# Keys and values of a fused decoder layer computed units ahead into a ring of six places

## The reference, cut to what matters

```
q, k, v = x @ Wq.T + bq, x @ Wk.T + bk, x @ Wv.T + bv         # 16 heads of 16
scores  = q k / 4, causal; only the 32 largest of a row are kept
x = layernorm(x + softmax(kept scores) v @ Wo.T + bo)
h = relu(x @ proj_in[e].T)            # 8 experts, 256 -> 512, every token
o = h @ proj_out[e].T                 # 512 -> 256
x = layernorm(x + sum_e gate[token, e] * o[e])   # gate from ctx_512 and itok
xq = 4-bit rounding of (x @ hadamard); wq = ternary weight
x = layernorm(x + xq @ wq.T)
```

## Time and profile before

| what | value |
|---|---|
| median of 3 runs | 617.47 us (616.04 to 617.79) |
| the profiled execution, its own time | 619.88 us |
| its span, first to last instruction | 618.1 us |
| TensorE (PE) busy | 551.0 us, 89% |
| VectorE (DVE) busy | 474.8 us, 77% |
| ScalarE (ACT) busy | 386.5 us, 63% |
| GpSimd (POOL) busy | 343.9 us, 56% |
| mean granted TensorE clock | 0.943 |
| mean DMA rate | 32 GB/s |

### The profile page before, as it was taken

One profiled execution on the slowest core, in us unless ns is written; L12 is line 12 of the kernel. 1 busy time (PEld: TensorE's weight loads), 2 busy tenths in 40 slices (PEclk: granted clock), 3 DMA queues, 4 the chain that ended last, 5 costly groups with the idle time before them and its releaser, 6 DMA issues. The chain is left out here.

```text
span 618.1 us, 20334 instructions
## 1 busy us (share of the span) xinstructions
PE 551.0 (89%) x7156; PEld 472.0 (76%) x7156; DVE 474.8 (77%) x2995; ACT 386.5 (63%) x909; POOL 343.9 (56%) x336
## 2 busy tenths in 40 slices
PE   5577658999899999999999999999999999989942
PEld 3455537888688888888888888888888888878831
DVE  1788988986888978798879887998799897543213
ACT  2677648676567566666767576766585767546520
POOL 2477555764447454754556455655554656656831
PEclk9967568999999999999999999999999999999985
DMA  8153330001000100002000100020001000000000
GB/s 243 37 181 116 108 103 2 3 2 53 3 2 3 46 26 3 3 3 70 3 1 21 53 3 2 3 71 1 3 3 54 3 3 1 20 1 2 19 0 17
DMA packets 20021, 19.88 MB, mean 32 GB/s; under 512 B 1744, under 2 KB 17872, under 8 KB 19920
## 3 DMA queue, kind: packets, MB, share of 16 engines
q1 hardware_dynamic: 19920, 18.59, 9.6%
HBM read 16.49 MB, written 2.10 MB: 30 GB/s over the span
## 5 line engine op out<-in xcount | busy, mean ns | idle before, releaser
L462 POOL TENSOR_TENSOR h_lo<-h_raw,h_hi 128x512 f16<-128x512 f32 x128 | 149.4, 1168 | 153.8 <-ACT h_raw L580 153.3
L769 PE MATMUL ps_o<-w_hi,h_lo 128*128 128x256 f16 x512 | 139.8, 273 | 5.2 <-POOL h_lo L462 3.6
L753 PE MATMUL ps_z<-x1t_hi,w_lo 128*128 128x256 f16 x512 | 140.4, 274 | 0.6 <-DVE x1t_lo L911 0.6
L753 PE MATMUL ps_z<-x1t_lo,w_hi 128*128 128x256 f16 x512 | 140.1, 274 | 0.0
L753 PE MATMUL ps_z<-x1t_hi,w_hi 128*128 128x256 f16 x512 | 140.0, 274 | 0.0
L769 PE MATMUL ps_o<-w_lo,h_hi 128*128 128x256 f16 x512 | 139.6, 273 | 0.0
L769 PE MATMUL ps_o<-w_hi,h_hi 128*128 128x256 f16 x512 | 139.6, 273 | 0.0
L855 DVE MATCH_REPLACE8 taken<-next,taken 128x48 f32<-128x48 f32 (+2 forms) x576 | 127.6, 233 | 0.2
L576 ACT ACTIVATE h_hi<-ps_z 128x512 f16<-128x512 f32 x128 | 75.9, 593 | 57.3 <-PE ps_z L753 56.4
L850 DVE MAX8 next<-taken 128x8 f32<-128x48 f32 (+2 forms) x576 | 95.9, 235 | 0.1
L483 POOL TENSOR_TENSOR acc<-go_sb,acc 128x512 f32<-128x512 f32 x56 | 71.1, 1270 | 35.9 <-ACT go_sb L590 35.7
(11 more groups left out here) (106 smaller groups left out, 993.5 us busy)
## 6 DMA issues: line engine op xcount, KB each, us to landing
w_raw<-in_w1t SPq DMA_DIRECT2D x8, 512.0 KB, 4.1
w_raw<-in_w2t SPq DMA_DIRECT2D x8, 512.0 KB, 5.2
xt_sb<-in_xt SPq DMA_DIRECT2D x8, 256.0 KB, 3.2
x_sb<-in_x SPq DMA_DIRECT2D x8, 256.0 KB, 3.2
out<-out_sb SPq DMA_DIRECT2D x8, 256.0 KB, 2.1
ctx_sb<-in_ctx_w SPq DMA_DIRECT2D x8, 128.0 KB, 2.4
itok_sb<-in_itok SPq DMA_DIRECT2D x8, 128.0 KB, 2.5
wq_sb<-in_wqt SPq DMA_DIRECT2D x1, 256.0 KB, 2.9
```

What stands on the lines that cost most here:

```text
L462: nc.gpsimd.tensor_tensor(h_lo[:, e % 2, 2 * z:2 * z + 2, :], h_raw[:, z, :, :], h_hi[:, e % 2, 2 * z:2 * z + 2, :], ALU.subtract)\
L753: last = pe.matmul(ps_z[z][:, d * UT:(d + 1) * UT], w[:, e, c, at:at + P], x[:, c, :], start=n == 0, stop=n == len(terms) - 1)
L769: last = pe.matmul(ps_o[e % 2][:, b * D:(b + 1) * D], h[:, e % 2, c, b * SEQ:(b + 1) * SEQ], w[:, e, c, :], start=n == 0, stop=n == len(te ...
```

## The change

Keys and values get a ring of six places (`kt_sb[:, v % RING]`, `v_sb[:, v % RING]`). Their products for units 1 to 7 no longer stand at a fixed distance from their own unit, but at seven slots of their own (`AHEAD`), and read x from a new buffer `xa_sb` with a transfer of its own, `load_xa`. `xt_sb` serves q, and k and v of unit 0. To make room, three buffers are shared: `had_sb` with `out_sb`, `ffn_sb` with `x2`, `f_sb` with `rounded`; two waits are added for that. All four tables of slots have new numbers. Cut to its core:

```diff
+RING = 6
...
 STEADY = {
-    "select": 2, "pace": 1, ... "k": -7.75, "copy_k": -8.75, "v": 3.25, "copy_v": 3.25,
-    "ln1_stats": 40.25, "ffn_scale": 86.5, ...
+    "select": 2, "pace": 0.75, ... "k": 24, "copy_k": -14.5, "v": 10, "copy_v": 34.5,
+    "ln1_stats": 39.5, "ffn_scale": 88.5, ...
 FIRST = STEADY | {
-    "scores": -3.75, "v": 10, "k": -6.25, "out_proj": 40, "ln1_stats": 41, "copy_ot": 38.5, "rstd1": 38.25, ...
+    "scores": -3, "v": -4.25, "k": -5.75, "copy_ot": 35.25, "rstd1": 37.75, "h_low": -3.5, ...
 PREP = {
-    "load_w": 10.75, "w_squares": 0.25, "w_sum": 2.25, "w_scale": 3.75, "w_high": 3.5, "w1_low": 3.75,
-    "w2_low": 5.5, "ffn_abs": -6.25, "ffn_sum": 26, "ffn_ternary": 42.25,
+    "load_w": 14.5, "w_squares": 0.75, "w_sum": 1.5, "w_scale": 2.75, "w_high": 3.75, "w1_low": 1,
+    "w2_low": 5.25, "ffn_abs": -8.25, "ffn_sum": 1, "ffn_ternary": 43.5,
+}
+AHEAD = {
+    "load_xa": 6.25, "k": -0.25, "copy_k": -0.25, "v": 0.75, "copy_v": 1.25, "at1": 10, "at2": 13.75, "at3": 17.5,
+    "at4": 24.5, "at5": 43.5, "at6": 55, "at7": 117.75,
 }
...
+AHEAD_STEPS = (("sp", "load_xa"), ("pe", "k"), ("act", "copy_k"), ("pe", "v"), ("act", "copy_v"))
...
         for engine, name in UNIT_STEPS:
-            put(base + at[name], engine, name, v)
+            if v == 0 or (engine, name) not in AHEAD_STEPS:
+                put(base + at[name], engine, name, v)
+        if v > 0:
+            for engine, name in AHEAD_STEPS:
+                put(AHEAD[f"at{v}"] + AHEAD[name], engine, name, v)
...
-        had_sb = sb("had_sb", [P, CD, D])
-        ffn_sb = sb("ffn_sb", [P, CD, D])
-        xt_sb = sb("xt_sb", [P, CD, UT])
+        xt_sb, xa_sb = sb("xt_sb", [P, CD, UT]), sb("xa_sb", [P, CD, UT])
-        kt_sb = sb("kt_sb", [P, GROUPS, UT])
+        kt_sb = sb("kt_sb", [P, RING, GROUPS, UT])
-        v_sb = sb("v_sb", [P, UB * HEADS, VW])
+        v_sb = sb("v_sb", [P, RING, UB * HEADS, VW])
+        had_sb, ffn_sb = out_sb, x2
-        f_sb = sb("f_sb", [P, UB, D])
+        f_sb = rounded
...
+                elif name == "load_xa":
+                    wait(sp, k_ready, v if v > 1 else 0)
+                    wait(sp, v_ready, v if v > 1 else 0)
+                    sp.dma_start(xa_sb[:, :, :], rows(xt)[:, :, v * UT:(v + 1) * UT]).then_inc(s_xa, 16)
...
-            nc.gpsimd.memset(v_sb[:, :, DH:VW], 1.0)
+            nc.gpsimd.memset(v_sb[:, :, :, DH:VW], 1.0)
...
+                elif name == "copy_k":
+                    act.wait_ge(k_ready, v + 1)
+                    wait(act, s_ready, TILES * (v - RING + 1))
...
                 elif name == "copy_v":
                     act.wait_ge(v_ready, v + 1)
-                    wait(act, pv_ready, TILES * v)
+                    wait(act, pv_ready, TILES * (v - RING + 1))
...
                 elif name == "ln2_apply":
+                    if v == 0:
+                        dve.wait_ge(ffn_prep, 3)
...
                 elif name == "quantise":
+                    wait(dve, t3_ready, v)
```

More of the change, by code:

```diff
@@ L101 @@
 STEADY = {
[L102 to L106, removed]
@@ L107 @@
-    "rstd1": 38.75, "ln1_apply": 42, "turn_x1": 41.75, "x1t_high": 40, "x1t_low": 42.5, "gate_scale": 45.75,
-    "experts": 44, "relu": 0, "h_low": 0, "gate_out": -0.5, "gated_add": -1, "ln2_stats": 77.75, "rstd2": 77.25,
[3 rows of a table removed]
+    "shift0": 1.25, "shift1": 0, "shift2": 1.75, "shift3": -1, "scores": -6.5, "copy_scores": -6.25, "exp": 5.5,
+    "select": 2, "pace": 0.75, "keep": 7.25, "turn_probs": 8.5, "copy_probs": 6.75, "turn_probs2": 9.25,
+    "copy_probs2": 9.5, "attend": 12.25, "normalise": 13.25, "load_xt": -12.5, "q": -13.5, "copy_q": -12.75,
@@ L112 @@
+    "spread_q": -11.5, "k": 24, "copy_k": -14.5, "v": 10, "copy_v": 34.5, "load_x": 16, "load_ctx": 33.25,
+    "x_plus_bo": 15.75, "gate_sums": 30, "turn_o": 37, "copy_ot": 36.5, "out_proj": 38.75, "ln1_stats": 39.5,
+    "rstd1": 38.75, "ln1_apply": 42, "turn_x1": 41.75, "x1t_high": 42, "x1t_low": 43, "gate_scale": 46.5,
+    "experts": 44, "relu": 0, "h_low": 0, "gate_out": 0.5, "gated_add": 0.5, "ln2_stats": 77, "rstd2": 77.5,
[3 rows of a table added]
 }
 FIRST = STEADY | {
-    "experts": 42.5, "shift1": 1.5, "relu": 0.5, "gate_out": 3, "shift2": 0.5, "copy_ot": 38.5, "shift0": 3,
@@ L115 @@
[L115 to L119, removed]
@@ new lines @@
+    "turn_o": 36.5, "exp": 6.25, "copy_q4t": 84.5, "copy_k": -5.25, "x2t_high": 78.25, "normalise": 12.5,
+    "quantise": 83.5, "load_xt": 3.5, "store": 124, "gate_scale": 48.75, "x1t_low": 42.5, "x2t_low": 82,
+    "turn_q4": 86, "ln2_apply": 81.75, "ln2_stats": 76, "load_x": 20.25, "rstd2": 77, "copy_probs2": 9.75,
+    "hadamard": 80.75, "copy_ot": 35.25, "spread_q": -14.5, "q": -16.5, "ffn_residual": 89.75, "copy_q": -9.75,
+    "load_ctx": 29.25, "ln3_stats": 97, "ffn": 88, "ln1_apply": 41.75,
@@ L122 @@
 }
 SECOND = STEADY | {
[L124 to L128, removed]
@@ L129 @@
-    "turn_x1": 41.25, "copy_k": -8.25, "exp": 4.75, "turn_probs2": 9.5, "gated_add": -2, "ffn_residual": 91.25,
-    "copy_probs": 8, "quantise": 83, "x1t_high": 40.5,
+    "shift2": -1, "copy_scores": -4.75, "select": 4.5, "pace": 0.5, "copy_probs": 8.75, "ln1_apply": 42.5,
+    "h_low": -0.5, "ffn": 90.25, "ffn_scale": 90, "spread_q": -14, "copy_q4t": 87.5, "ln1_stats": 41, "keep": 6.75,
[3 rows of a table added]
+    "gate_scale": 46.25, "rstd1": 36.75, "copy_v": 41.75, "gate_sums": 31.75, "quantise": 82, "load_xt": -10.5,
@@ L131 @@
+    "gated_add": -1, "copy_k": -20.25, "to_q4": 84.75, "k": 19, "turn_probs2": 9,
 }
 LAST = STEADY | {
[L133 to L136, removed]
@@ L137 @@
[L137 to L139 removed]
+    "shift2": 0, "normalise": 11.75, "x_plus_bo": 20.25, "gate_sums": 31.5, "experts": 43.75, "copy_probs": 8.75,
+    "turn_probs2": 9, "shift1": 0.25, "copy_k": -11, "ffn": 94.75, "out_proj": 38.5, "attend": 13.5, "to_q4": 87.25,
@@ new lines @@
+    "rstd2": 76.75, "copy_scores": -6, "ffn_residual": 78.5, "exp": 5, "ffn_scale": 88, "turn_o": 37.25,
+    "turn_x2": 77.5, "copy_q4t": 89.25, "ln3_stats": 99.25, "copy_v": 32, "rstd1": 39.25, "store": 116.25,
+    "ln1_apply": 41, "ln2_apply": 76.75, "quantise": 85.25, "ln2_stats": 71.5, "v": 11.75, "load_xt": -11.75,
+    "gate_scale": 49.75, "x2t_high": 82.5, "spread_q": -13.5, "rstd3": 98.75, "keep": 7.75, "copy_q": -12.25,
+    "ln1_stats": 37.5, "hadamard": 81.5, "k": 25, "x2t_low": 81.25, "gate_out": -0.5,
```

64 lines of the change are left out of this document (35 added, 29 removed), and 9 rows, old and new, of tables (SECOND, STEADY).

## The result

| | before | after |
|---|---|---|
| median (lowest to highest), 16 runs each | 618.47 us (615.64 to 619.89) | **612.28 us** (609.66 to 616.04) |
| the profiled execution (span) | 619.88 us (618.1) | 610.15 us (608.4) |

The ratio is 0.9905 with a 95% interval of 0.9889 to 0.9922: the changed kernel is 5.9 us faster.

A forecast was written before the change was run, and what follows sets the result against it. TensorE was taken to bound the steady stretch (busy 61.44 of 62 us), VectorE's selection chain most of the start. Terms +3.7 + 5.8 - 3.9 + 1.6 - 11.0 = -3.8 us gave 613.7 us against 617.47; own range 611 to 616, wider 606 to 621.

The forecast's parts named there:

- the likeliest case: Whole kernel: the forecast's own sum, 613.7 us, with a range of 611 to 616; chance 0.37.
- Start, first step: Up to the first scores: v.0 moves ahead of them uncovered, +3.7 us; first scores at 18.8 us instead of 15.14.
- Start, middle: Between scores.0.1 and attend.0.2: six more projections, partly covered by 14.3 us of TensorE idle time, +5.8 us (0 to +11.7).
- Start, end: From keep.0.3 to the end of ln1_apply: 21.8 us against 25.7, -3.9 us, with the apply at 0.74 us.
- Period 0: Unit 0's experts: two more projections on TensorE, partly filling its idle time, +1.6 us (0 to +3.4).
- Periods 1, 3, 4 and 5: Steady periods: two projections fewer each, -11.0 us in all; bounds 1.1 and 3.44 us a period.
- At nothing: Added x transfers, ones set in v_sb, waits for shared buffers and the ring: claimed to cost nothing.
- the early clock: Rival, start: TensorE at full level from the second tile, middle free, chain products shorter; 607.9 down to 605.5 us; chance 0.25.
- The pile-up: Rival, between scores.0.1 and attend.0.2: TensorE stays at 1.2 GHz, +11.7 instead of +5.8; 619.6 up to 622 us; chance 0.20.
- VectorE taking over: Rival, steady periods: only 1.1 us won in each of four, -4.4 instead of -11.0; 620.3 us; chance 0.10.

The follow-up runs named there:

- e3: The changed kernel with v of unit 0 back behind the second scores and second w_sum instead of ahead of the first scores; 614.45 us, ratio 0.9942.
- e5: e1 with ffn_scale moved to 88.5, behind the last select stage and the next tile's first_max; 636.34 us, ratio 1.0293.
- e4: The changed kernel with k and v of units 5, 6 and 7 back in the periods before their use; 620.17 us, ratio 1.0035.
- e7: The changed kernel with k and v of units 1 to 4 each computed twice into the same place; 624.93 us, ratio 1.0090.
- e2: The changed kernel's new tables, but k and v of units 1 to 7 in their old places, one unit ahead; 633.97 us, ratio 1.0252.
- e6: The changed kernel with ffn_scale ahead of the last select stage again and ffn a third of a slot earlier; 628.08 us, ratio 1.0158.
- e12: The changed kernel with eight unused products of a constant ahead of q.0; 610.73 us in five runs, ratio 0.9868.
- e1: The changed kernel's early products and ring, with the tables of before but for a slot or two; 656.84 us, ratio 1.0623.
- e8: The changed kernel with k and v of unit 7 at slot 90 instead of 117.75, in period 1; 613.67 us, ratio 0.9922.
- e9: The changed kernel with k and v of unit 4 moved from the start to period 0; 613.67 us, ratio 0.9923.
- e11: e5 with the weight loads (load_w in PREP) issued 3.75 slots later; 635.86 us, ratio 1.0274.
- e10: The changed kernel with k and v of units 3 and 4 moved from the start to period 0; 616.47 us, ratio 0.9971.

## Why the prediction was right, and where it wasn't

The sum said -3.8 us and the medians -5.9; the likeliest case, its own range of 611 to 616 and the mechanism (products leave the full periods, the start pays) held. In the start one term was wrong and another right by luck. By its own steps:

*Start, first step, +3.7:* wrong. The first scores came at 15.07 us, not at 18.8. The step took v.0 at 3.76 us from where it stood before, behind idle time. Right behind q.0 and k.0 it took 1.97, and k.0 itself 1.99 instead of 3.78. That k.0 was fast is not the change: its level differs between executions. With k.0 at one level the early v.0 does put off the first scores, by 1.8 us (13.30 in e3, 15.07 here) or 2.0 (14.88 in e5, 16.89 in e4). The 18.8 is what an execution shows in which TensorE is still at the lower level: 18.43 in e7, where k.0 took 3.78 and v.0 3.57. For the whole kernel, as e3 shows, the move is worth -2.3 us, not +3.7.

*Start, middle, +5.8 (0 to +11.7):* right in size, by luck. keep.0.3 came at 71.51 us, 5.1 later than before, and 5.2 counted from the first scores. But the terms are others. The forecast had 16.3 us of projections and 3.8 of handovers, less 14.3 of idle time filled. Measured between the first scores and keep.0.3: TensorE's projections take 11.3 us more (22.7 instead of 11.3; three of the nine near the lower level, 3.4 to 3.8 us, six at the full one), the same other products as before take 5.6 us less (16.2 instead of 21.8), since the clock was granted 0.84 instead of 0.77, and the idle time stayed at 18.6. Against e2, which has the new tables without the early products and 21.9 us idle there, 3.3 us were filled. So the cover of 14.3 us was not there, and e7 too, with eight more projections, left 18.6 us idle. What made up for it was the clock, which the forecast counted for the projections alone. e7 prices further projections there at 1.4 us, nearer the full level's 1.72 than the lower one's 3.7. In these executions a denser queue went with a higher clock for its neighbours, so the price of one product, at either level, is not the cost of adding it.

*Start, end, -3.9:* right. From keep.0.3 to the end of the apply it was 25.7 us and is 21.6 (71.51 to 93.11): -4.1. The apply took 0.73 us, as said.

The three together: the first expert product came at 96.31 us instead of 94.77, +1.5 where +5.6 was forecast; of the missing 4.1, 3.8 are the first step.

*Period 0, +1.6 (0 to +3.4):* +0.2 by the sums in the profiled pair, +0.1 by x1t_lo, but +1.6 to +1.8 in the four executions of e3, e6, e7 and e12, whose period 0 has the same order. The term was right in size, as far as one trace of before can tell: TensorE is idle 3.3 us less than before in this period and, in those four, busy 4.9 us longer. The two projections are 3.4 of the 4.9; the rest was not taken apart. Read from the profiled pair alone the two would look free.

*Periods 1, 3, 4 and 5, -11.0:* right in size. Together -12.8 by the sums and -9.9 by x1t_lo. Where both landmarks nearly agree, a period won 1.7 to 1.9 (period 3) and 2.5 (period 4), against -2.75 forecast. Its reason was right (ffn_scale's place fills VectorE's wait), but its lower bound was not: with the old order I expected to keep 1.1 us a period. e6 shows a loss of 0.9 to 1.8 us in periods 3 to 5 against before, and e1 of 2.7 to 3.5. In e6 a TensorE with less work waits 3.3 us a period for keep, which it hardly did before (0.2), and the price of the wrong order is then more than the work removed. Why the chain through VectorE comes out longer than it was before is not shown.

*At nothing:* held for the transfers (at most 1.14 us of waiting for an x transfer in the start), the constants and the shared buffers' waits.

Of the rivals, the early clock was half there: the products on the chain got shorter as it said, but the middle was not free. The pile-up did not come, since TensorE did not stay at its lower level. VectorE taking over, with turn_probs waiting for keep, is e6.

## What to carry to other kernels

Work moved off a bounding engine pays only if the engine next in line can follow. Look in its timeline for one fixed wait a period, and move what waits behind other ready work; here that one place was worth more than the move. Idle time is a stock of which only a part can be filled: in period 0 3.3 of 7.7 us, in the middle of the start 3.3 of 21.9, and what comes after costs its full time. So ask what an idle stretch waits for before counting it as cover. And compare a stretch in several executions before calling work free: one profiled pair showed period 0 1.5 us too short.

## What the runs showed of the hardware

The level at which TensorE starts differs between executions of one order of work. q.0 always took 3.5 to 3.8 us without work ahead of it, but k.0, 0.93 us behind it, took 1.99 us (2.00 in e6) in the changed kernel and in e1, e2, e3, e6, e8, e9 and e11, 3.78 us in before, e4, e5 and e7, and 3.62 us in e10. The Trainium skill, page "TensorE: Matmul & The Clock Gate", section "What's actually happening", says the same of a kernel's first products, that the number of slow ones is not the same in every run.

The granted clock doesn't show it there. Stretch of e7 in which q.0 (from 5.51 us) took 3.78 us, the lower level, at a granted clock of 1.00; then its k.0:

```profile
5.00:10.00 5.00, 3.78 (x8) 2.53 (x8) 0.00 (x0) 1.13 (x4) 0.00 (x0) 1.00 0.89 242
```

```profile
10.22 3.78 PE L654 MATMUL ps_misc<-xt_sb,wk_sb 128*128 128x256 f32 x8 [0.93 <-ACT qt_sb L530]
```

In the first microseconds the level is to be read from the duration of a known product, not from the clock column. The level differs at the first expert products too: the full one in the changed kernel's trace, the lower one in the other 13.

The first apply on VectorE took 3.42 us before, while GpSimd lowered a weight (88.66 to 91.98 us); in the changed kernel that step was over at 91.13 us, and the apply, from 92.38 on, took 0.73 us. The traces show more of it. The two traces have 96 halves of such applies, of all three layer norms (128x256, one instruction each). 17 of them start while GpSimd is in an elementwise step; they take 1.02 to 1.36 us and end 0.15 us after that step, or in one case after the next one. Of the other 79, 78 take 0.39 to 0.41 us; the last, 2.28 us, starts 0.02 us ahead of a GpSimd step of 2.12 us. The slow halves are 5 before and 12 in the changed kernel, so the new order pays for this in other places. No run tried it by itself.
